# The state chain of a gated delta-rule kernel in full 128x128 matmuls: decay-corrected keys and queries side by side as weights, the update accumulated in PSUM, block-diagonal operands

## The reference

```python
def step(S, inp):                     # S: 128 x 128 state
    qt, kt, vt, gt, bt = inp          # k, q l2-normed after a short convolution and silu
    S = S * gt[..., None]             # a decay for each of the 128 key channels
    pred = jnp.einsum('bhk,bhkv->bhv', kt, S)
    delta = (vt - pred) * bt[..., None]
    S = S + kt[..., None] * delta[:, :, None, :]
    o = jnp.einsum('bhk,bhkv->bhv', qt, S)
    return (S, o)
```

## Time and profile before

| | |
|---|---|
| median of 3 runs | 2618.57 us (2617.99 to 2619.50) |
| profiled execution, its own time | 2619.83 us |
| its span, first to last instruction | 2618.0 us |
| TensorE busy | 2441.7 us (93%) |
| VectorE busy | 2122.1 us (81%) |
| ScalarE busy | 1408.8 us (54%) |
| GpSimd busy | 1273.1 us (49%) |

### The profile page before, as it was taken

One profiled execution on the slowest core, in us unless ns is written; L12 is line 12 of the kernel. 1 busy time (PEld: TensorE's weight loads), 2 busy tenths in 40 slices (PEclk: granted clock), 3 DMA queues, 4 the chain that ended last, 5 costly groups with the idle time before them and its releaser, 6 DMA issues.

```text
span 2618.0 us, 102732 instructions
## 1 busy us (share of the span) xinstructions
PE 2441.7 (93%) x46512; PEld 1462.9 (56%) x46512; DVE 2122.1 (81%) x3249; ACT 1408.8 (54%) x2647; POOL 1273.1 (49%) x989
## 2 busy tenths in 40 slices
PE   6799999999999999999999999989899898998989
PEld 3466666666666666666666666664333333333333
DVE  3778888888989888989899888863349999999981
ACT  3555555555655565566566655542465646455332
POOL 0556555555555555655555555540035645545530
PEclk8899999999999999999999999999999999999999
DMA  1000000000000000000000000010023323333320
GB/s 55 23 10 14 14 23 14 13 14 14 24 14 14 14 24 14 14 14 24 13 14 17 21 14 14 7 58 1 26 74 99 130 92 126 106 105 121 129 85 16
DMA packets 52069, 105.61 MB, mean 40 GB/s; under 512 B 7084, under 2 KB 11948, under 8 KB 51376
## 3 DMA queue, kind: packets, MB, share of 16 engines
q1 hardware_dynamic: 51632, 99.04, 11.5%
HBM read 96.65 MB, written 2.37 MB: 38 GB/s over the span
## 4 chain that ended last, share of the span: by engine, by line
PE 77%; DVE 11%; issue 6%; ACT 4%; POOL 1%; DMA 0%; SPq 0%; DVEq 0%; ACTq 0%
PE bank L381 13%; PE bank L483 7%; DVE hs L1705 6%; PE bank L446 5%; PE bank L631 4%; PE bank L1522 4%; PE pair L599 4%; PE pair L589 3%; PE bank L571 3%; PE bank L605 2%; PE bank L544 2%; PE bank L553 2%; PE bank L415 2%; PE pair L1444 2%; PE bank L594 2%
## 5 line engine op out<-in xcount | busy, mean ns | idle before, releaser
L673 DVE SCALAR_TENSOR_TENSOR cv<-raw,taps,cv 128x1024 f32<-128x1024 f32 x288 | 407.0, 1422 | 16.0 <-ACT cv L939 14.7
L2011 POOL TENSOR_TENSOR dBu<-dtu,Bn 128x1024 f32<-128x1024 f32 x128 | 306.1, 2393 | 229.5 <-DVE hc L1712 224.6
L381 PE MATMUL bank<-xn,W 128*128 128x512 f32 x768 | 378.3, 616 | 0.0
L938 ACT ACTIVATE raw<-bank 128x512 f32<-128x512 f32 x192 | 114.7, 598 | 401.3 <-PE bank L381 400.3
L1522 PE MATMUL bank<-hc,eye 128*128 128x512 f32 x512 | 255.1, 627 | 56.7 <-DVE hc L1712 56.6
L1909 ACT ACTIVATE bank<-dtv,m_A 128x512 f32<-128x512 f32 x256 | 174.4, 687 | 210.1 <-DVE hs L1705 209.4
L1198 POOL TENSOR_TENSOR kL<-kL,tot 128x512 f32<-128x512 f32 x128 | 199.8, 1561 | 163.3 <-PE bank L446 162.2
L381 PEld LDWEIGHTS bank<-xn,W 128*128 128x128 f32 x768 | 137.4, 192 | 135.1 <-issue 131.2
L1522 PEld LDWEIGHTS bank<-hc,eye 128*128 128x128 f32 x512 | 93.9, 195 | 206.6 <-DVE hc L1712 116.8
L1712 DVE TENSOR_TENSOR hc<-hs,Cn 128x1024 f32<-128x1024 f32 x128 | 172.8, 1350 | 7.9 <-PE bank L1522 3.7
L1200 POOL TENSOR_TENSOR R<-R,tot 128x512 f32<-128x512 f32 x128 | 165.3, 1291 | 0.0
(11 more groups left out here) (267 smaller groups left out, 5579.2 us busy)
## 6 DMA issues: line engine op xcount, KB each, us to landing
Bn<-ssm_rows SPq DMA_DIRECT2D x128, 256.0 KB, 3.5
Cn<-ssm_rows SPq DMA_DIRECT2D x128, 256.0 KB, 3.2
W<-in_head_w SPq DMA_DIRECT2D x32, 448.0 KB, 3.4
WO<-in_out_w SPq DMA_DIRECT2D x32, 192.0 KB, 2.4
xT<-in_xT SPq DMA_DIRECT2D x1, 2048.0 KB, 8.0
out_xT<-xT SPq DMA_DIRECT2D x4, 512.0 KB, 3.7
xn<-in_w_gate SPq DMA_DIRECT2D x1, 1024.0 KB, 6.5
xn<-in_w_up SPq DMA_DIRECT2D x1, 1024.0 KB, 8.3
```

Of the source, the lines that this page charges most:

```text
L381: m = pe.matmul(psum[bank][:, :], w[:, (kind * KT + k) * P:(kind * KT + k + 1) * P], xn[:, k, b, cols], start=k == 0, stop=k == KT - 1)
L673: dve.scalar_tensor_tensor(cv[m % 2][:, :, :], raw[m % 2][:, :, i:i + SEG], taps[:, h, KQV[n], i:i + 1], cv[m % 2][:, :, :], MUL, ADD).the ...
L2011: pool.tensor_tensor(dBu[at % AHEAD][:, :, :], dtu[s][:, half * DT2:(half + 1) * DT2, :], spread(Bn[at % DEEP][:, :], 1, DT2), MUL).then_i ...
```

## The change

The product W S (pred) and the output of a chunk come from one pair of full matmuls. The tile `RW` holds, for each chunk, the keys' operand R, W of batch 0 beside q of batch 0, and q of batch 1 beside W of batch 1, so that `W_and_q` is a 128x128 weight for each batch; its product with S goes into that batch's own bank `CHAIN[b]`: W's rows to `rows_of(b)`, q's to the other half, `out_rows(b)`. For that the two batches change places in the projections (`1 - b`). The update u = Y v is no longer a stage of its own: it opens the accumulation in `CHAIN[b]` for four chunks at a time (16 matmuls a unit, weights of 64 rows x 128 columns), W is negated when it is copied, and PSUM then holds D itself. D is copied to the two diagonal blocks of `Dd` (batch 0 by ScalarE, batch 1 by VectorE), and one matmul (weights 128x128, 256 moving columns) makes both outer products. Y is spread to a block-diagonal `Y128` by four ScalarE copies in place of GpSimd's multiplication by a mask (L1229), and W comes from eight 128x128 matmuls. Squares and gate are now done for each batch's half of the partitions, so twice as many instructions. `vT` has two buffers and not three. `PLACES`, `FRONT_AT` and `EARLY_AT` are new lists. The operations on R have the chunk as an axis of its own in their access patterns.

```diff
 PLACES = [
-    (-1, [61.85, 106.12, 122.1, 139.6, 143.3, 146.82]),
-    (0, [21.81, 40.36, 47.08, 47.36, 53.47, 57.55]),
-    (0, [46.86, 50.32, 55.67, 60.17, 65.32, 67.24]),
-    (0, [67.41, 72.3, 76.47, 103.16]),
-    (0, [60.56, 60.56, 63.8, 85.34, 91.54, 94.81, 107.86]),
-    (0, [84.11, 95.7]),
-    (0, [99.66, 99.66, 107.96, 112.78, 118.5, 118.87, 125.56, 130.82, 136.85, 136.85, 148.79, 151.57, 172.94,
-         176.87, 184.71]),
-    (1, [25.31, 33.14, 37.11, 39.91, 40.97, 44.26, 44.94, 50.25, 50.25, 53.23, 53.5, 60.5, 69.14, 77.16, 80.34,
-         82.32, 82.59, 90.86, 90.86, 98.95, 99.79]),
-    (1, [90.68, 91.07, 93.46, 132.71]),
-    (2, [7.01, 7.01, 7.01]),
-    (2, [28.71, 37.38]),
-    (2, [11.53, 13.37, 18.08, 20.17, 22.91, 25.81, 34.31, 37.82, 39.88, 44.95, 48.7, 52.78, 59.34, 63.88, 69.27,
-         76.49, 78.59, 81.97]),
-    (2, [37.83, 42.52, 89.16, 90.28, 90.28, 91.85, 91.85, 110.22, 112.87, 112.87, 116.57, 121.42, 172.93]),
+    (-1, [67.2, 100.23, 125.16, 134.34, 146.71, 148.37]),
+    (0, [25.39, 47.77, 47.77, 47.77, 54.5, 56.52]),
+    (0, [48.69, 51.06, 59.59, 64.77, 69.62, 70.53]),
+    (0, [69.72, 72, 75, 91.73]),
+    (0, [57.75, 60.54, 75.61, 81.23, 90.64, 95.12, 261.13]),
+    (0, [82.11, 92.08]),
+    (0, [95.18, 95.18, 105.96, 109.96, 118.24, 118.24, 129.23, 133.45, 138.96, 146.34, 148.79, 155.73, 170.28,
+         175.89, 175.89]),
+    (1, [28.6, 32, 34.2, 42.98, 43.32, 48.24, 48.24, 49.31, 50.26, 52.05, 55.76, 61.21, 62.28, 76.42, 76.42, 84.48,
+         84.48, 91.24, 91.24, 95.77, 95.77]),
+    (1, [88.5, 90.61, 92.34, 116.43]),
+    (2, [5.12, 5.34]),
+    (2, [27.77, 36.62]),
+    (2, [7.98, 9.84, 12.45, 17.79, 23.3, 27.64, 30.27, 33.29, 37.28, 40.76, 48.69, 48.69, 50.52, 54.79, 58.01,
+         62.53, 72.02, 75.33, 79.52, 79.52]),
+    (2, [36.9, 43.43, 86.5, 89.42, 89.42, 90.66, 90.66, 98.73, 98.73, 110.63, 116.97, 121.65, 173.17]),
 ]
...
@@ hybrid_block @@
-        vT = [sa(f"vT{i}", [P, NC, P]) for i in range(3)]
-        WT = [sa(f"WT{i}", [P, NC, P]) for i in range(2)]
+        RW = [sa(f"RW{i}", [P, NC, 3 * P]) for i in range(2)]
+        vT = [sa(f"vT{i}", [P, NC, P]) for i in range(2)]
+        Dd = sa("Dd", [P, 4, NB, P])
...
+        def W_and_q(s, c, b):
+            return RW[s][:, c, (1 + b) * P:(2 + b) * P]
+        def out_rows(b):
+            return rows_of(1 - b)
...
@@ solved, TensorE @@
                     if q == 0:
                         pe.wait_ge(*off_kept.at(g))
-                        pe.wait_ge(*vT_set.at(g, 1))
+                        pe.wait_ge(*kRT_set.at(g, 1))
                     for c in range(4 * q, 4 * q + 4):
-                        for b in range(NB):
-                            m = pe.matmul(psum[bank][rows_of(b), (c % 4) * P:(c % 4 + 1) * P],
-                                          Y64[rows_of(b), c, :, :].rearrange("p h i -> p (h i)"), vT[g % 3][rows_of(b), c, :])
-                    m.then_inc(u_full.sem)
...
-                for c in range(NC):
-                    for b in range(NB):
-                        m = pe.matmul(psum[w_banks[b]][:, c * CH:(c + 1) * CH], kRT(g)[rows_of(b), c, :],
-                                      Y64[rows_of(b), c, :, :].rearrange("p h i -> p (h i)"))
+                        o = psum[bank][:, :].rearrange("p (b c t) -> p b c t", b=NB, t=CH)[:, :, c % 4, :]
+                        m = pe.matmul(o, kRT(g)[:, c, :], Y128[:, c, :].rearrange("p (b t) -> p b t", b=NB))
...
@@ state, TensorE @@
+                    if c % 4 == 0:
+                        if c:
+                            pe.wait_ge(*og_set.at(g, 0))
+                        else:
+                            if g:
+                                pe.wait_ge(*og_set.at(g - 1, 1))
+                            pe.wait_ge(*off_kept.at(g))
+                            pe.wait_ge(*vT_set.at(g, 1))
+                        for c4 in range(4):
+                            for b in range(NB):
+                                m = pe.matmul(psum[CHAIN[b]][:, c4 * P:(c4 + 1) * P], Y128[rows_of(b), c + c4, :],
+                                              vT[s][rows_of(b), c + c4, :], start=c4 == 0, stop=False,
+                                              skip_group_check=True)
+                        m.then_inc(u_full.sem)
+                        yield
...
                     for b in range(NB):
-                        m = pe.matmul(psum[CHAIN[0]][rows_of(b), 0:P], WT[s][:, c, rows_of(b)], src[:, b, :])
+                        m = pe.matmul(psum[CHAIN[b]][:, o_cols], W_and_q(s, c, b), src[:, b, :], start=False, stop=False,
+                                      skip_group_check=True)
                     m.then_inc(pred_full.sem)
-                    if c == 4:
-                        pe.wait_ge(*og_set.at(g, 0))
-                    for b in range(NB):
-                        pe.matmul(psum[OUT][rows_of(b), (c % 4) * P:(c % 4 + 1) * P], R[s][:, 1, c, b, :], src[:, b, :],
-                                  start=c % 4 == 0, stop=False, skip_group_check=True)
-                    yield
-                    pe.wait_ge(*d_set.at(g, c))
-                    for b in range(NB):
-                        m = pe.matmul(psum[CHAIN[b]][:, P:2 * P], kT[s][rows_of(b), c, :], vT[g % 3][rows_of(b), c, :])
-                    m.then_inc(outer_full.sem)
+                    yield
+                    pe.wait_ge(*d0_set.at(g, c))
+                    pe.wait_ge(*d1_set.at(g, c))
+                    pe.matmul(outer, kT[s][:, c, :], Dd[:, c % 4, :, :]).then_inc(outer_full.sem)
                     yield
...
@@ turn_v, VectorE @@
+                        if g >= 2:
+                            dve.wait_ge(*u_full.at(g - 2, 1))
...
@@ state, VectorE @@
+                    if c == 4:
+                        dve.wait_ge(*within_full.at(g, 0))
+                    elif c == 0 and g:
+                        dve.wait_ge(*within_full.at(g - 1, 1))
                     dve.wait_ge(*pred_full.at(g, c))
-                    dve.tensor_tensor(vT[g % 3][:, c, :], vT[g % 3][:, c, :], psum[CHAIN[0]][:, 0:P],
-                                      SUB).then_inc(d_set.sem)
+                    dve.tensor_copy(Dd[rows_of(1), c % 4, 1, :],
+                                    psum[CHAIN[1]][rows_of(1), c % 4 * P:(c % 4 + 1) * P]).then_inc(d1_set.sem)
...
@@ output, VectorE @@
-                    dve.wait_ge(*o_squared.at(g, hh))
+                    for b in range(NB):
+                        dve.wait_ge(*o_squared.at(g, 2 * hh + b))
+                        m = dve.scalar_tensor_tensor(og[out_rows(b), 4 * hh:4 * hh + 4, :],
+                                                     th(g)[out_rows(b), 4 * hh:4 * hh + 4, :], 1.0,
+                                                     psum[CHAIN[b]][out_rows(b), :].rearrange("p (c v) -> p c v", v=P),
+                                                     ADD, MUL)
...
@@ inverse, ScalarE @@
+                act.wait_ge(*y_set.at(g, NL - 1))
+                for w in range(4):
+                    m = act.activation(Y128[quad(w), :, y_cols(w)], XY[quad(w), 1, :, :], ACT.Copy)
+                m.then_inc(y_spread.sem)
...
@@ solved, ScalarE @@
-                    act.activation(vT[g % 3][:, 4 * q:4 * q + 4, :].rearrange("p c d -> p (c d)"), psum[bank][:, :],
-                                   ACT.Copy).then_inc(u_set.sem)
...
@@ state, ScalarE @@
+                    act.wait_ge(*pred_full.at(g, c))
+                    act.activation(Dd[rows_of(0), c % 4, 0, :], psum[CHAIN[0]][rows_of(0), c % 4 * P:(c % 4 + 1) * P],
+                                   ACT.Copy).then_inc(d0_set.sem)
...
@@ output, ScalarE @@
-                    for c in range(4 * hh, 4 * hh + 4):
-                        m = act.activation(og[:, c, :], psum[OUT][:, (c % 4) * P:(c % 4 + 1) * P], ACT.Square,
-                                           accum_out=osum[:, c:c + 1])
+                    for b in range(NB):
+                        for c in range(4 * hh, 4 * hh + 4):
+                            m = act.activation(og[out_rows(b), c, :], psum[CHAIN[b]][out_rows(b), (c % 4) * P:(c % 4 + 1) * P],
+                                               ACT.Square, accum_out=osum[out_rows(b), c:c + 1])
...
```

More of the change, by code:

```diff
@@ L249, in hybrid_block, with y_cols @@
         view = psum[PROD][:, :].rearrange("p (c a i) -> p c a i", c=NC, a=2)
-        outer = pair[:, :].rearrange("p (b n) -> p b n", b=NB)[:, :, P:2 * P]
+        outer = psum[OUTER][:, 0:NB * P].rearrange("p (b v) -> p b v", b=NB)
+        R, W_of = [], []
+        for t in RW:
+            both_parts = t[:, :, :].rearrange("p c (a x) -> p a c x", a=2)
+            R.append(both_parts[:, :, :, 0:P])
+            W_of.append(both_parts[:, :, :, P:P + CH])
+        def W_and_q(s, c, b):
+            return RW[s][:, c, (1 + b) * P:(2 + b) * P]
+        def out_rows(b):
+            return rows_of(1 - b)
+        def y_cols(w):
+            return slice(SUBB * w, SUBB * (w + 1))
         def kRT(g):
@@ L745, in products @@
```

(33 more changed lines are left out.)

143 lines of the change are left out of this document (71 added, 72 removed), and 24 rows, old and new, of the table FRONT_AT.

## The result

The changed kernel takes 2708.62 us (median of 4 runs, 2702.72 to 2713.04) against 2618.28 for the kernel before, a ratio of 1.0337 with a 95% interval of 1.0323 to 1.0352. It is 90 us slower; the forecast was 2605, and 2637 was the end of the range.

The account below looks back on a forecast made before the run. TensorE's list of groups was taken to bound the attention. -23 us from its list, +10 for new waits, zero for the tail and a little less fetching made -14 us: 2605 us for the median, range 2582 to 2637.

Parts of the forecast that it names:

- What bounds the kernel: Attention lasts as long as TensorE's list of groups, 52.5 us a unit, with little waiting; TensorE busy 97 to 98.5%.
- Changes of shape and TensorE's parts: TensorE in attention: replaced work grows 0.55 us a unit, fewer shape changes save neighbours 1.28, net -0.73.
- the 23 us: Forecast gain on TensorE's list in the attention: 0.73 us a unit, times 32 units.
- Rival 3: TensorE's 64x128 pairs of u don't overlap: 3.4 us, +0.5 a unit, 2645 us with waits; chance 0.08.
- That rule against the change: Outer product: 64-row tiles up to twice as fast, so zeros in `Dd` could cost +80 us over 256 chunks.
- Other engines: ScalarE gains at most 5.6 us a unit; VectorE keeps some 5 us of slack in 52; nothing on the path.
- Thin cover: Late D and u behind the squares, in attention: 0.3 us a unit taken, +10 us in all.
- Tail zero: Tail after the attention: same steps in another order, 8 us either way of 798, taken as zero.
- The second: Attention: D late by a ScalarE instruction and u waiting for squares eat the gain, 1.3 us a unit, 2637; chance 0.25.
- The fifth: VectorE's slack in the attention is too small: gain under 10 us, 2615 to 2619; chance 0.05.
- Rival 4: New order also removes TensorE's idle time in the attention, some 0.55 us a unit, 18 us more: 2587; chance 0.14.
- The slower outcomes together: Whole kernel slower than before: 0.15 from new waits plus 0.08 from pairs of u not overlapping, chance 0.23.

Follow-up runs that it names:

- e9: Changed kernel with the dots' last step (`bs`) late again and both copies of D on ScalarE: 2653.39 us.
- e6: Changed kernel with both copies of D on VectorE, none on ScalarE: 2749.36 us.
- e7: Changed kernel with the first tap of each convolution on VectorE cut to 2 of 512 columns, all handoffs kept: 2704.24 us.
- e1: Changed kernel with one place different, the dots' last step (`bs`) late again: 2697.07 us.
- e4: Changed kernel with the old lists of places, steps for u fitted in, the feed-forward list left new: 2735.2 us.
- e11: Changed kernel without three of batch 1's four squares in each half of the output: 2700.21 us.
- e13: Changed kernel with one number changed, the products' third step moved from 105.96 to 109.9: 2766.43 us.
- e14: Changed kernel with the products' third step at 109.9, both copies of D on ScalarE and the dots' last step late: 2725.32 us.
- e15: Kernel before with only the new lists FRONT_AT and EARLY_AT: 2629.5 us.
- e3: Kernel before with all new lists of places, the two steps for u left out: 2949.44 us.
- e10: Changed kernel with GpSimd's `bm` computed in full in the first unit alone: 2715.31 us.

## Why the prediction was wrong

**What bounds the kernel.** Right for the kernel before. The attention did last as long as TensorE's list, but only because every exchange with VectorE arrived inside its cover, and I took that as nearly given for new places.

**Changes of shape and TensorE's parts.** Right for each group, and not shown for the sum. u starts 1.09 us before the next group per half (forecast 1.0 to 1.1), pred with q S 0.44 to 0.64, mostly 0.55, and the outer product 0.43 to 0.63; L624 and L618 show it above (1189.31 to 1189.82, 1186.76 to 1187.31). W takes 1.98 for 1.9. The changes of shape in TensorE's list are 52 and 36 a unit, as counted. Whether the list shrank by the forecast 0.73 us a unit stays open: by the shortest distances it did by 1.3 us in the kernel after, by 0.6 in e9 and not at all in e6, which have the same TensorE order; by busy time over both stretches it didn't (51.4 before, 51.6 after). No form shows the 23 us in its time. Rival 3 is out. The Trainium skill's table (TensorEngine Tiling (Array Packing), section Theoretical Speedup) has tiles of 64 rows up to twice as fast. That rule against the change did not bite: an outer product is nowhere near 0.84 us.

**Other engines.** ScalarE has 502.6 us in 800, 34.4 a unit, against 30.9 before: 3.6 more, less than 5.6. D in halves costs VectorE 0.295 us, a little more than the whole D of 128 partitions before (0.280); I had 0.25. Zeroing, the swapped batches and the new axis cost nothing: the shortest L785 on `tot` is 0.69 us, as L759 was 0.68. Their means did grow, from 0.84 to 1.15 us, and no run shows what for. "That leaves it some 5 us of slack" was the wrong kind of number: e7 shows that an engine's idle share says neither that it is the bound nor that it isn't. And I had not sorted the other engines' lists: in them `bs` moves ahead of `tot`, which makes up 1.9 of the 5.3 us a unit that VectorE's busy time grew by (46.1 before, 51.4 after, 49.5 in e1). That was readable before the run, though it is worth only 12 us by e1, barely clear of noise.

**Thin cover: the step that failed.** "I take 0.3 us a unit", with a bound of 1.5, measured 2.2 to 3.6. The bounds were drawn from two places, D in ScalarE and u behind the squares. ScalarE's D is not among the kernel after's long waits (in e4 it is, 19.0 us); the squares are worth 8 us (e11). What came instead is VectorE's in-order list: D, S, Sx and the inverse's XY stand in fixed places between operations of 0.7 to 2.9 us that themselves wait for TensorE (L467) or GpSimd. I compared the distance from pred to the outer product on TensorE and not what VectorE has between the same two. Taking VectorE's D away gives 42 us, and with a late `bs` 55, 61% of the loss; adding one takes 41. Making the run on VectorE later (e13, e14) takes 58 and 72 more, because then the state is behind it. The other 39% stay open.

**The sum.** -23 + 10 was to be -13 us. Measured is 2.34 x 31 = +72 us in the units: 2.2 to 3.6 us of waiting, and for the list between 0.2 us more and 1.3 less. The 14.5 us without a cause at L483 are 3.8 at L504 after; that fetching was behind them, as the sum has it, no run shows. Tail zero, with 8 either way: measured +9.5, in the passage to the tail, and e15 shows that the places can make it.

**The rivals.** The second had the mechanism (D late, u waiting) with 1.3 us a unit, about half of what came, and the wrong engine. Its sign, above 30 us of waiting for ScalarE's D or for u's banks, was not met on TensorE's matmuls (1.4 us, for u's banks); its weight loads, which run ahead of them, waited 24.0 and 6.7 us. The fifth's sign was met (93.7% and 93.4%) and its story is false. Rival 4's gain does not show. The slower outcomes together had a chance of 0.23, and all of them ended at 2645 us or below.

**What stays open.** e9's profiled execution is still 32 us above the kernel before: 0.76 us a unit, some 23.5 us, and 11.8 behind the attention, less 2.9 at the start. Its waits at L529 (for ScalarE's Z) and L646 (for VectorE's `cen`), 19.2 us, are about as much as the units have lost, but no run takes them away. Whether places exist for this chain that beat the old one was not found; no version here does. Structure and places could not be told apart for the rest, since each half alone (e3, e4) does worse than both.

## What to carry to other kernels

Where two engines exchange small results through lists in fixed order, price a change by each handoff: for every one, what the *other* engine has between its arrival and its turn, with what those operations wait for. An engine's busy share decides nothing here: 3.3 us a unit less load gave 4 us in all, one 0.29 us copy a chunk gave 42. Sort the lists of all engines when places are redrawn, not only the one that bounds: one number moved for VectorE's sake (e13) also moved a group on TensorE that VectorE's run waits for. And try a hot copy on the engine that has no long run before moving it within its list, as the run has to stand in front of something.

## What the runs showed of the hardware

- The same 128x512 addition on VectorE took 0.68 us, or 2.93 us when GpSimd's 3.8 us multiplication had begun first; and without that block the kernel took 12 us less (e1) or 7 more (e10), as a wait for TensorE took its place.
- A copy from PSUM of 64 partitions by 128 takes VectorE 0.295 us and a square of 64x128 takes ScalarE 0.259, against 0.280 for a subtraction and 0.277 for a square of 128x128 in the kernel before (medians): half the partitions saved next to nothing here, so splitting by batch nearly doubled an operation's price.
- Pairs of 64x128 matmuls on two row halves overlap: 16 instructions of 128 columns (L605) took 1.09 us, 0.07 each, where the prediction worked out 0.11 for one on the full array; the pairs in L599, with their changes of shape, had left 0.1 or 0.2 us a pair open.
